# Wide bf16 products added to TensorE's queue ahead of two kinds of step in a three-block transformer layer on one core

## What is computed

```python
x = x + xattn(layernorm(x), ctx, ...)   # causal self attention, cross attention to 257 keys, ReLU feed-forward
x = x + delta(layernorm(x), ...)        # L = 2 layers over 4 batches of T = 256 tokens, 8 heads of 16
x = x + moe(layernorm(x), ...)          # 32 experts, the best 8 of each token, and a shared one

# one layer of delta, which is where the change lies
h = rmsnorm(x, norm1_w[l])
q, k = l2norm(silu(h @ Wq)), l2norm(silu(h @ Wk));  v = silu(h @ Wv);  beta = 2 * sigmoid(h @ Wb)
def step(S, inps):                      # for each token, S is 16 x 16 for every head
    pred = einsum('bhkv,bhk->bhv', S, ki)
    S = S + bi * ki[:, None] * (vi - pred)[None, :]
    return S, einsum('bhkv,bhk->bhv', S, qi)
o = rmsnorm(scan(step), onorm_w)        # a norm over each head's 16 features
x = x + o @ Wo
g, y = split(rmsnorm(x, norm2_w[l]) @ Wg)
x = x + silu(g) * y @ Wd
```

## Time and profile before

| what | value |
|---|---|
| time, median of 3 runs | 873.99 us (867.12 to 875.69) |
| time of the profiled execution | 878.75 us |
| its span, first to last instruction | 875.7 us |
| mean granted TensorE clock | 0.793 |
| TensorE matmul busy | 665.4 us, 76% of the span |
| VectorE busy | 492.0 us, 56% |
| ScalarE busy | 239.8 us, 27% |
| second block within the span, roughly | 183 to 617 us |

### The profile page before, as it was taken

How to read it: one execution, slowest core, us unless ns; L and a number is a source line. 1 busy time by engine, 2 the same in 40 slices (tenths; PEclk the granted TensorE clock), 3 DMA queues, 4 the chain that set the end, 5 groups by cost and what they waited for, 6 DMA issues and landing times.

```text
span 875.7 us, 16028 instructions
## 1 busy us (share of the span) xinstructions
PE 665.4 (76%) x6648; PEld 455.7 (52%) x6648; DVE 492.0 (56%) x1180; ACT 239.8 (27%) x529; POOL 93.7 (11%) x127
## 2 busy tenths in 40 slices
PE   3447377047479899987859948989559999689995
PEld 2234234025469799675648948866424444334442
DVE  4473853458765772465676873445574554754453
ACT  1112123055233033244325312124322122222221
POOL 1333315141000001011010001002200000100000
PEclk9668587667565775996958955799689999779998
DMA  9990000400000000000000000031000000100001
GB/s 351 296 368 0 24 0 0 72 1 1 1 2 2 1 3 2 1 2 1 1 1 2 4 1 2 1 93 62 0 1 0 1 0 0 24 0 0 0 0 24
DMA packets 13308, 29.51 MB, mean 34 GB/s; under 512 B 2272, under 2 KB 7008, under 8 KB 12992
## 3 DMA queue, kind: packets, MB, share of 16 engines
q1 hardware_dynamic: 13248, 28.64, 10.2%
HBM read 26.54 MB, written 2.10 MB: 33 GB/s over the span
## 4 chain that ended last, share of the span: by engine, by line
PE 61%; DVE 24%; DMA 3%; ACT 3%; issue 3%; POOL 3%; SPq 2%; DVEq 0%; POOLq 0%; ACTq 0%
PE psum L677 6%; PE psum L678 6%; PE psum L687 6%; PE psum L539 5%; PE psum L505 4%; PE psum L605 3%; PE psum L525 3%; PE psum L646 3%; PE psum L649 2%; POOL rstd L889 2%; DMA zlast<-in_ctx_last 2%; PE psum L612 2%; DVE mid L1189 2%; PE psum L485 2%; DVE rowv L1187 2%
## 5 line engine op out<-in xcount | busy, mean ns | idle before, releaser
L1309 DVE TENSOR_TENSOR mid<-psum,act_o 128x512 f32<-128x512 f32 x64 | 44.3, 692 | 89.9 <-PE psum L687 82.4
L410 PE MATMUL psum<-ident,yn 128*128 128x128 f32 x96 | 24.2, 414 | 85.2 <-DVE yn L969 46.0
L677 PE MATMUL psum<-yT,weg_sb 128*128 128x512 f32 x136 | 75.0, 634 | 6.5 <-DVE arena L1303 6.1
L870 ACT ACTIVATE act_o<-psum 128x512 f32<-128x512 f32 x64 | 38.2, 597 | 137.7 <-PE psum L680 137.7
L678 PE MATMUL psum<-yT,weu_sb 128*128 128x512 f32 x136 | 73.0, 620 | 0.0
L687 PE MATMUL psum<-mid,wed_sb 128*128 128x512 f32 x136 | 69.3, 595 | 4.7 <-DVE mid L1278 3.2
L410 PEld LDWEIGHTS psum<-ident,yn 128*128 128x128 f32 x96 | 17.0, 210 | 90.6 <-DVE yn L969 50.4
L720 ACT ACTIVATE arena<-psum 128x512 f32<-128x512 f32 (+1 forms) x60 | 35.6, 600 | 85.8 <-PE psum L505 37.3
L505 PE MATMUL psum<-arena 32*64 32x128 f32 x1024 | 43.8, 338 | 10.0 <-DVE XA L1162 4.4
L677 PEld LDWEIGHTS psum<-yT,weg_sb 128*128 128x128 f32 x136 | 26.9, 203 | 40.1 <-issue 31.4
L505 PEld LDWEIGHTS psum<-arena 32*64 32x64 f32 x1024 | 38.5, 171 | 15.3 <-ACT arena L720 5.3
(11 more groups left out here) (230 smaller groups left out, 1274.8 us busy)
## 6 DMA issues: line engine op xcount, KB each, us to landing
arena<-in_ctx_t SPq DMA_DIRECT2D x16, 514.0 KB, 8.1
arena<-in_ctx_z SPq DMA_DIRECT2D x16, 512.0 KB, 9.4
XA<-in_x SPq DMA_DIRECT2D x1, 1024.0 KB, 5.0
zlast<-in_ctx_last SPq DMA_DIRECT2D x4, 256.0 KB, 16.2
x_mid<-XA SPq DMA_DIRECT2D x2, 512.0 KB, 2.6
X<-x_mid SPq DMA_DIRECT2D x8, 128.0 KB, 4.8
weg_sb<-in_we_gate SPq DMA_DIRECT2D x2, 512.0 KB, 6.5
weu_sb<-in_we_up SPq DMA_DIRECT2D x2, 512.0 KB, 7.4
```

The costliest lines, as they stand in the source:

```text
L410: last = pe.transpose(bank[:, jj * D:(jj + 1) * D], src[u][:, jj, :], ident[:, :])
L677: pe.matmul(banks[4 * u][:, :], weg_sb[:, w, :], yT[u][:, :], start=True, stop=True)
L1309: dve.tensor_tensor(act_gu[u][:, :], banks[4 * u + 1][:, :], act_g[u][:, :], ALU.mult).then_inc(x_gu, 1)
```

## The change

A helper issues `count` products of 96 x 128 weights with 96 x 512 data, both from `spread` in bf16, into one PSUM bank with `start` and `stop` set; nobody reads the result. At `lout` of group 0 eight of them go ahead of the wait for `l_inv`, into the bank `b0` of group 1, which is read out by then. At `otr` of group 0 six of them go ahead of the wait for `o_n`, into the bank that the transposes write next; they wait for `s_ocp` of group 0, the copy out of that bank. There are four `lout` and four `otr`: 32 and 24 products. Nothing else is moved or removed.

```diff
+            def dense(bank, count):
+
+                for n in range(count):
+                    pe.matmul(bank, spread[:, 0:P], spread[:, 0:512], start=True, stop=True)
+
             for kind, l, pr in STEPS:
...
                     elif kind == "lout":
+                        if u == 0:
+                            dense(banks[bank + 2], 8)
                         pe.wait_ge(l_inv, pi + 1)
                         from_lanes(b1, pr, u).then_inc(l_omm[u], 1)
...
                     elif kind == "otr":
+                        if u == 0:
+                            pe.wait_ge(s_ocp[u], pi + 1)
+                            dense(b0, 6)
                         pe.wait_ge(o_n, i + 1)
                         transposes(b0, yn, g, o_tr)
```

## The result

| what | before | with the change |
|---|---|---|
| median | 871.51 us (20 runs, 865.44 to 878.14) | 867.38 us (20 runs, 859.35 to 872.59) |
| ratio, 95% interval | | 0.9936, 0.9909 to 0.9964 |
| time of the profiled execution | 878.75 us | 860.35 us |
| its span and mean clock | 875.7 us, 0.793 | 858.5 us, 0.823 |

The medians lie 4 us apart where 19 were forecast; the ratio stands for 5.6 us, 3 to 8 by its interval. Medians are over all runs, while ratios leave out those more than 1.5% above the fastest of their kernel. The two profiled executions lie 18 us apart, since that of before is slower than all 20 runs of its kernel and that of the change is among the fastest of its own.

The account below looks back on a forecast made before the run. TensorE, 61% of the chain, was taken to bound the kernel, with long gapless stretches at half clock. -5.5 - 10 - 2.3 - 4 - 1 = -22.8 from the profiled 878.75 gave 856; forecast 855 us, range 838 to 871.

Parts of the forecast that it names:

- Step 1: `lout` of A0: the eight cost 3.5 us but raise the clock for the products behind; -5.5 us, +3.5 if it stays low.
- the other branch: At `lout` of A0, the case that the clock rises: L516 of B comes earlier, a gain of 7.4 us, taken as -5.5.
- Step 2: `lout` of B0 and `otr` of A0: the clock stays high through L525 and L539; -10 us, bounds +3.5 and -14.5.
- Step 3: `lout` of A1: eight cost 0.6 us beyond the gap, L525 and L561 run faster; -2.3 us, bounds +0.6 and -3.
- Step 4: `lout` of B1: the idle 2.57 us covers the eight, L525 and L539 run faster; -4 us, bounds 0 and -9.
- Step 5: The other `otr`: 0 at B0 and A1; at B1 L410 and L633 may run at the higher clock, -1 us.
- the first: Rival: gaps behind ACT's and DVE's copies lower the clock after each L525; 867 with one stretch held, 877 with none; chance 0.22.
- The second: Rival: products of mostly zero weights do not move the clock and only cost; +8 us, 882 by the median; chance 0.09.

Follow-up runs that it names:

- h2: The change with its eight products at `lout` of A0 taken from dense bf16 data on 128 rows; 858.74 us, ratio 0.9869 to the kernel before.
- h3: The change with its eight products at `lout` of A0 taken from dense bf16 data on 96 rows; 862.42 us, ratio 0.9869 to the kernel before.
- e1_b0_only: The kernel before with only the eight products at `lout` of B0 added, none at any `otr`; 861.68 us, ratio 0.9906.
- the two repeats: The change run again unaltered, for a second and a third profile; medians 868.26 and 861.25 us, ratios 0.9939 and 0.9894 to the kernel before.
- f1_fill: The kernel before plus eight products at `lout` of B0, twelve at A1, sixteen at B1, none at A0 or any `otr`; 854.86 us, ratio 0.9813.
- f2_all_full: The kernel before plus 16, 8, 12, 16 products at `lout` of A0, B0, A1, B1 and six at `otr` of B1; 849.76 us, ratio 0.9727.
- g1_best: The kernel before plus 12, 8, 12, 16 products at the four `lout`, six at B1's `otr`, four between B1's L525 and L539; 840.74 us, ratio 0.9652.
- h1_best_fp32: g1_best with the twelve bf16 products at `lout` of A0 replaced by two fp32 ones; 838.07 us, ratio 0.9624 to the kernel before.

## Why the prediction was wrong

The time, 867.38, lies inside the range of 838 to 871, but the gain is 4 us instead of 19. By its steps:

1. **Step 1 (A0, -5.5) failed.** "If they raise the clock by then" did not come true: in three profiles of the change L525 takes 7.0 us behind the eight. Measured +3.5, the bound named for that case. The working behind the other branch was right: once raised, L516 of B comes 11.0 us sooner behind L525 (22.8 for 33.8), less 4.7 us for twelve, or 3.1 for two fp32, which makes -6.3 and -7.9 where 7.4 stood; h2's eight bf16 on 128 rows give -7.2. What failed was to take eight of these products as enough. Why they are not is open: their 96 rows or their length, since the rise came 4.0 us or later behind the first such product wherever it came, or the zeros among them, though h3's dense data did no better.
2. **Step 2 (B0, -10) held in its mechanism, and in size partly by luck.** L525 at 3.9 us, L646 20 us behind it ("some 21"), at full clock in all three profiles; in all fifteen profiles with eight at B0 the stretch from L525 to `wo` is 67.5 to 68.3 us. In the change it is 68.3 against 84.0, 74.8 and 76.2: a mean of -10.0, or -8.3 with the 1.7 us of delay. But the working took 84.0 as what stood to be won, and could not know that the clock comes back earlier in other executions; the bound of -14.5 was never to be had in the median. The number taken was right because of a discount given for another reason, small gaps in the changed kernel. The six at A0's `otr` were taken as covered but cost 0.8 us and bring nothing: without them (e1_b0_only and four others) L646 comes 19.2 us behind L525 instead of 20.0.
3. **Step 3 (A1, -2.3) failed.** The eight run 1.8 us into a gap of 2.6 to 2.8, the 0.7 to 0.9 us left cost the clock within L525, and the stretch to `lin` of B1 is 51.0 us as before. The step counted the gap of 1.22 behind the earlier trace rows, but at full clock the L561 ahead end earlier than in that execution. With twelve L525 takes 3.9 and the stretch 47.8: 3.2 us, the bound.
4. **Step 4 (B1, -4) failed** likewise: 1.5 to 1.9 us stay open behind the eight, L539 takes 13.8 us. "The idle time covers the eight whole" was right and was the fault: eight end before the wait does, and at A1 and B1 the clock fell wherever they did. Sixteen and four give 60.1 to 49.1, 11 us, more than the 9 of the bound.
5. **Step 5 (-1) held in part.** B1's `wo` takes 2.05 us instead of 3.1 to 3.5 in all three profiles of the change. In the two repeats the clock falls behind it (the next L656 takes 2.0 and 2.1 us for 1.1), and from `wo` of B1 to the third block's L666 (L676 in the change) it is 40.1 us, where it is 38.5 in the first and 39.5 to 39.9 before. The six at A1 bring nothing; those at B0 may cost, as said below.

Means of three profiles each, by stage: +0.3 us ahead of A0, +3.5 at A0, +1.7 and -10.0 at B0, -1.6 between `wo` of B0 and L525 of A1, 0 at A1, -0.9 from L525 of B1 to the third block. That is -7.0, as the mean of the three spans goes from 871.3 to 864.3; the medians differ by 4.1. Of the 15.8 us that this lacks to the sum of -22.8, 9.0 are step 1, 3.3 step 4, 2.3 step 3 and 1.7 the delay at B0.

The stretch between `wo` of B0 and L525 of A1 has no step of its own but moves by 3 us. It is 55.0 us in the first profile of the change and 58.4 in the two repeats, where the clock falls once more behind that `wo`. Of the ten profiles with B0 held and the six at B0's `otr`, nine have 58.4; of the five with B0 held and without them (e1_b0_only, f1_fill, f2_all_full, g1_best, h1_best_fp32), four have 55.1 to 55.3 and one 58.1. So these six may cost 3 us in most runs, which would be part of why e1_b0_only has the lower median than the change; no run has them alone taken out.

The rivals: the first, gains taken back by waits, has 867 as its number, which is what came, but partly by luck. It lets the clock fall in the gaps behind ACT's and DVE's copies; at A1 and B1 it fell already in the gap ahead of L525, the wait for `l_inv`, and the copy's gap counted only once that one was filled (f1_fill, f2_all_full). Nor do its sums start from one place: 867 is 10 less than an 877 that comes from the profiled 878.75, while -8 from the median is 866. It was given 0.22 and held to be the less likely since 7.6 us of L539 kept the clock; that row has no gap in it. The second was right for A0 alone (+3.5).

One reading of the rows was too hopeful. The 37.4 us at full clock are not "the same kinds of products" as the slow stretches: some 19 us of them are the wide products of L646, L649, L655 and L561, of which the three slow ones together hold 4.7 us. The rule of the Trainium skill ("TensorE: Matmul & The Clock Gate", "What's actually happening"), that busyness gives the clock back, is again not borne out where it stood against the change: 33.8 us of gapless small products at 0.50 in every profile without a raise at A0, and full clock 2.5 to 5.9 us behind the first wide one where it rose.

## What to carry to other kernels

Before costing a lost clock, take more than one profile of the same kernel: where the clock comes back by itself varies, and one execution may show twice the loss of the next. Here products that hold the clock had to reach to the end of the wait, and the next wait had to be filled too, even one of 0.66 us. Products ahead of work that is already slow have to raise the clock or they are only cost; find the count by trying, and look at several profiles, since the point of the rise moves by microseconds. When TensorE gets faster, look for the copy that it now waits for, since here the clock was lost there next.

## What the runs showed of the hardware

- Behind a single wait of 0.66 us between two rows of small products the clock was low for 20 us; with four wide products in it the whole of 49 us ran at 1.00.
- Eight bf16 products in 3.5 us did not raise the clock in three profiles with 96 rows of mostly zeros and in one with 96 dense rows; behind eight on 128 dense rows it rose in the one profile taken, and with two fp32 products, in 3.1 and 3.7 us, in both.
- Within twelve and sixteen of the 96-row products it did rise, in two profiles each, 4.0 to 5.9 us behind the first. With 128 rows it was 2.5 to 4.7 us.
- An fp32 product of 512 columns shows as two MATMUL records and costs 0.86 us at full clock, as much as four bf16 ones of 0.22; four took 6.0 us where the clock rose among them.
- The last round of the third block takes 124.6 to 124.7 us in all profiles, though its first 30 us run at a clock of 0.5 to 0.8 each time; the spread of some 13 us between runs of one kernel lies ahead of it, for the change in the stages named above.
